# The last mixture of experts: scattered copies of token rows, or token numbers and gathers

## The reference

```python
NUM_EXPERTS, TOP_K, N_GROUPS, N_LIMITED_GROUPS = 32, 6, 4, 2
scores = jax.nn.sigmoid(x @ gate_w)                       # 2048 x 32
# the best 2 of 4 groups of 8 experts, then the best 6 experts in them
_, selected_experts = jax.lax.top_k(masked_scores, K)
weights = take_along_axis(original_scores, selected_experts)
weights = weights / weights.sum(-1)
xs = x_exp[argsort(selected_experts.ravel())]             # 12288 (token, choice) pairs, by expert
g = ragged_dot(xs, w_gate, group_sizes)                   # 256 -> 176
u = ragged_dot(xs, w_up, group_sizes)                     # 256 -> 176
d = ragged_dot(silu(g) * u, w_down, group_sizes)          # 176 -> 256
out = d[unsort_idx].reshape(T, K, H)
expert_out = sum(out * weights[..., None], axis=1)
shared = (silu(x @ sw_gate) * (x @ sw_up)) @ sw_down      # a dense expert, 352 wide, for all tokens
return expert_out + shared
```

## Time and profile before

| what | value |
|---|---|
| median of 3 runs | 3175.97 us (3175.49 to 3180.71) |
| the profiled execution's own time | 3173.69 us |
| its span, from first to last instruction | 3171.7 us |
| mean granted PE clock | 0.891 of full speed |
| busy: PE, DVE, ACT, POOL | 83%, 61%, 49%, 28% of the span |
| last feed-forward: first load issued | 2609.97 us |
| slots ready, first scatter of the dispatch | 2648.88 us |
| last scatter of the dispatch issued | 2769.39 us |
| first transpose of the tile loop | 2820.16 us |
| last addition of products issued | 3143.08 us |
| last DVE addition to x begins, takes | 3159.12 us, 4.43 us |

### The profile page before, as it was taken

The page is one execution under the profiler, slowest core; times in us unless marked ns, Lnnn a source line. Parts: engine busy times, 40 slices in busy tenths (PEclk is TensorE's granted clock), DMA queues, the critical chain, the costliest instruction groups (busy, mean ns, idle before and its releaser), DMA issues. The chain is left out here.

```text
span 3171.7 us, 64439 instructions
## 1 busy us (share of the span) xinstructions
PE 2641.8 (83%) x19747; PEld 2209.5 (70%) x19747; DVE 1937.4 (61%) x5951; ACT 1549.9 (49%) x4650; POOL 901.1 (28%) x800
## 2 busy tenths in 40 slices
PE   6885984899976599999948599999999984279995
PEld 5663553666654499999936499999999982157774
DVE  5666324787762688788843577777777773035553
ACT  6874222899971455555543344444444442013331
POOL 2111784111101322222244201001010114726664
PEclk9995755999986699999979799999999997589998
DMA  6003555900010111010024333332333326446776
GB/s 185 2 14 125 89 93 147 313 2 2 2 42 0 60 41 51 28 57 34 21 111 137 130 105 101 100 104 81 104 101 100 89 67 271 148 113 121 123 125 141
DMA packets 188015, 291.72 MB, mean 92 GB/s; under 512 B 29921, under 2 KB 158105, under 8 KB 183937
## 3 DMA queue, kind: packets, MB, share of 16 engines
q1 hardware_dynamic: 148800, 226.07, 22.2%
q0 software_dynamic: 38976, 62.68, 10.2%
HBM read 110.55 MB, written 94.22 MB: 65 GB/s over the span
## 5 line engine op out<-in xcount | busy, mean ns | idle before, releaser
L584 PE MATMUL bank<-norm_t_high,w 128*128 128x256 f32 (+1 forms) x2176 | 446.8, 287 | 8.3 <-DVE w L766 8.3
L732 ACT ACTIVATE probs<-bank,neg_max 128x256 f32<-128x256 f32 (+1 forms) x512 | 224.9, 444 | 394.0 <-DVE inv L841 385.9
L584 PEld LDWEIGHTS bank<-norm_t_high,w 128*128 128x128 f32 x2176 | 363.2, 194 | 8.9 <-issue 8.9
L1150 ACT ACTIVATE probs<-neg_scores,bound 128x256 f32<-128x256 f32 (+1 forms) x768 | 366.9, 486 | 3.3 <-DVE bound L1221 2.9
L584 PE MATMUL bank<-norm_t_low,w 128*128 128x256 f32 (+1 forms) x1088 | 310.0, 285 | 0.0
L1221 DVE CUSTOM_DVE_ANT_0 neg_scores<-bank,table 128x256 f32<-128x256 f32 (+1 forms) x768 | 261.7, 397 | 63.3 <-PE bank L1062 63.3
L870 POOL TENSOR_TENSOR summed<-turned 128x512 f32<-128x512 f32 x64 | 82.6, 1291 | 710.0 <-DVE turned L792 710.0
L2197 POOL DMA_INDIRECT sums<-shared,norm_t x127 | 198.2, 1560 | 176.1 <-ACT shared L2017 79.7
L642 PE MATMUL bank<-k,q 128*128 128x256 f32 (+1 forms) x1536 | 244.6, 295 | 0.0
L847 DVE SCALAR_TENSOR_TENSOR x_sb<-bank,inv,x_sb 128x256 f32 (+1 forms) x512 | 224.3, 480 | 24.3 <-DVE inv L841 14.1
L740 ACT ACTIVATE probs_t<-bank 128x384 fp32r<-128x384 f32 (+1 forms) x256 | 139.7, 546 | 201.1 <-PE bank L652 200.6
(11 more groups left out here) (394 smaller groups left out, 6012.3 us busy)
## 6 DMA issues: line engine op xcount, KB each, us to landing
z<-norm_t_high SPq DMA_DIRECT2D x96, 256.0 KB, 2.5
z<-norm_t_low SPq DMA_DIRECT2D x96, 256.0 KB, 2.5
rows<-blank SPq DMA_DIRECT2D x1, 21336.0 KB, 65.0
norm_t<-rows SPq DMA_DIRECT2D x127, 168.0 KB
q_turned<-halves SPq DMA_DIRECT2D x256, 64.0 KB
k_turned<-halves SPq DMA_DIRECT2D x256, 64.0 KB
staged<-in_attention SPq DMA_DIRECT2D x12, 1280.0 KB, 6.6
weights<-in_experts SPq DMA_DIRECT2D x1, 13376.0 KB
```

The source lines that it names most:

```text
L584: ins = nc.tensor.matmul(out, stationary(a), moving(c), start=(kt == 0 and m == 0), stop=(kt == n - 1 and m == 2))
L732: ins = nc.scalar.activation(probs[j % 2][:, t, 0:width], s_bank[j % 2][:, score_columns(causal, t)], ACT.Exp, bias=neg_max[j % 2][:, t:t ...
L1150: ins = nc.scalar.activation(probs[q % 2][g][:, t, 0:width], neg_scores[g][:, t, 0:width], ACT.Exp, bias=bound[q % 2][:, g, t:t + 1], scal ...
```

## The change

The last feed-forward gets a stage of its own, `gathered_stage`, in which no token row is copied to its places. The normalised rows, with slot numbers and gates (again 336 floats), are stored once, in token order, by one DMA of SP. One-hot rows are multiplied on PE, as in layer 0, over 127 tiles, and give for each slot the token (`gather_ids`) and the row of the result (`row_ids`, which is choice x 2048 + token; slots without a token get a spare row). Because the row needs the choice too, there are four numbers per tile and not three, and POOL computes the fourth. The shared expert is split: two `shared_up` steps lie before the routing's products on PE, five more and two `shared_down` steps lie between the 16 token tiles of the one-hot products, and five and two come behind. In the loop POOL gathers each tile's rows (six to seven tiles ahead, 8 buffers) and writes products without addition to seven regions of 2048 rows (six choices and a spare one). At the end six results are loaded and added, not two. Fewer expert weights come early (15 of 32 experts, not 22), as the routing's tables are larger; PE waits for the rest only at tile 15. The blank tables of layer 3 are no longer written. The diff, cut:

```diff
-    narrow_attention_stage(core, narrow[1], ..., blanks=scratch[3])
+    narrow_attention_stage(core, narrow[1], ...)
-              3: SparseExperts(32, 6, 176, True, ACT.Silu, "limited", 127, 352, 2, 5)}
+              3: SparseExperts(32, 6, 176, True, ACT.Silu, "limited", 127, 352, True, 12)}
-        sparse_feed_forward(3)
+        gathered_feed_forward(3)
+
+def gathered_stage(core, cfg, router_in, weights_in, shared_in, tables_in, scratch):
+    RING, OUT_RING, AHEAD, MATCHES = 8, 8, 6, 3
+    NUMBERS = 4
+    UP_BESIDE, DOWN_BESIDE = {0: 2, 2: 3, 7: 4, 9: 5, 11: 6}, {4: 0, 13: 1}
+    ACTIVATED_BESIDE, GATED_BESIDE, ADDED_BESIDE = {3: 2, 5: 3, 9: 4, 12: 5, 14: 6}, {4: 2, 6: 3, 10: 4, 13: 5, 15: 6}, {8: 0}
+    def last_steps(up, down):
+        for work, at in ((up, 7), (up, 8), (up, 9), (down, 2), (up, 10), (up, 11), (down, 3)):
+            work(at)
...
+            def _(sp):
+                sp.wait_ge(rows_ready, 1)
+                sp.wait_ge(row_normed, TILES)
+                sp.dma_start(scratch.rows.rearrange("(p t) r -> p t r", p=P), rows).then_inc(table_stored, 16)
+                sp.wait_ge(table_stored, 16)
+                sp.dma_start(weights[:, rows_at:E * W], weights_in[:, rows_at:E * W]).then_inc(weights_loaded, 16)
+                sp.wait_ge(ids_ready, 1)
+                sp.wait_ge(s_y_done, 2 * CHUNKS)
+                sp.dma_start(weights[:, early_weights:rows_at], weights_in[:, early_weights:rows_at]).then_inc(weights_loaded, 16)
+                sp.wait_ge(y_done, NT)
+                for e in range(NT - OUT_RING, NT):
+                    sp.wait_ge(sent_back[e % OUT_RING], landed(e))
+                for k in range(TOP):
+                    sp.dma_start(results[k], ...).then_inc(results_loaded[k], 16)
...
+                # PE
+                for t in range(TILES):
+                    pe.wait_ge(placed, t + 1)
+                    pe.wait_ge(numbered, t + 1)
+                    pe.wait_ge(ordered, t + 1)
+                    for k in range(TOP):
+                        ins = nc.tensor.matmul(ids_bank, of_place[t % MATCHES][:, k, :], of_tile[t % MATCHES][:, :, k, :], ...)
+                    ins.then_inc(sorted_in, 1)
+                    if t in UP_BESIDE:
+                        shared_up(UP_BESIDE[t])
+                    if t in DOWN_BESIDE:
+                        shared_down(DOWN_BESIDE[t])
+                last_steps(shared_up, shared_down)
...
+                # ACT
+                    act.wait_ge(matched, t + 1)
+                    nc.scalar.activation(of_tile[t % MATCHES][:, 0, :, :], of_tile[t % MATCHES][:, 2, :, :], ACT.Copy, scale=columns[:, 0:1])
+                    nc.scalar.activation(of_tile[t % MATCHES][:, 1, :, :], of_tile[t % MATCHES][:, 2, :, :], ACT.Copy, scale=float(t))
...
+                # DVE
+                    need(dve, sorted_in, t - MATCHES + 1)
+                    nc.vector.scalar_tensor_tensor(of_tile[t % MATCHES][:, 2, :, :], ..., ALU.add, ALU.is_equal).then_inc(matched, 1)
+                    nc.vector.tensor_tensor(of_place[t % MATCHES], ..., ALU.is_equal).then_inc(placed, 1)
...
+                # POOL
+                for t in range(TILES):
+                    pool.wait_ge(matched, t + 1)
+                    nc.gpsimd.tensor_tensor(of_tile[t % MATCHES][:, 3, :, :], of_tile[t % MATCHES][:, 2, :, :], order_bf.to_broadcast([P, TOP, NT]), ALU.mult)
+                pool.wait_ge(table_stored, 16)
+                pool.wait_ge(ids_ready, 1)
+                for n in range(NT + AHEAD):
+                    if n < NT:
+                        if n < RING:
+                            pool.wait_ge(s_up_done, SB * (n // KT + 1))
+                        need(pool, product_ready, n - RING + 1)
+                        nc.gpsimd.indirect_dma_start(tile_rows[n % RING], None, scratch.rows, bass.IndirectOffsetOnAxis(gather_ids[:, n:n + 1], 0))
+                    e = n - AHEAD
+                    if e >= 0:
+                        pool.wait_ge(product_ready, e + 1)
+                        nc.gpsimd.indirect_dma_start(scratch.results, bass.IndirectOffsetOnAxis(row_ids[:, e:e + 1], 0), product[e % OUT_RING], None)
```

More of the change, by code:

```diff
@@ L1646, with __init__ @@
 class SparseExperts:
-    def __init__(self, experts, top, hidden, gated, act, router, tiles, shared, sums, crowded):
+    def __init__(self, experts, top, hidden, gated, act, router, tiles, shared, gathers, crowded):
         self.E, self.top, self.H, self.gated, self.act = experts, top, hidden, gated, act
-        self.router, self.tiles, self.shared, self.sums, self.crowded = router, tiles, shared, sums, crowded
+        self.router, self.tiles, self.shared, self.crowded = router, tiles, shared, crowded
+        self.gathers = gathers
         self.width = self.part_width(hidden)
[L1657 to L1661, removed]
+        self.used = C + 1 + 2 * experts if gathers else C + 2
+        self.row = -(-self.used // 16) * 16
+        self.id_at = C
     def part_width(self, hidden):
@@ L1690, in write_blanks @@
         .then_inc(scratch.blank_rows, 16)
[L1691 to L1698, removed]
+    sp.wait_ge(scratch.blank_rows, 16)
+    sp.dma_start(scratch.rows[:, cfg.id_at].rearrange("(i p) -> p i", p=P).bitcast(I32), core.blank_ids[:],
+                 allow_slow_non_contiguous=True).then_inc(scratch.blank, 16)
 class Arena:
@@ L1725, in sparse_stage @@
     nc, x, bank, E, H, TOP = core.nc, core.x, core.bank, cfg.E, cfg.H, cfg.top
-    NT, ROW, W, SUMS, COPIES = cfg.tiles, cfg.row, cfg.width, cfg.sums, cfg.copies
+    NT, ROW, W, COPIES = cfg.tiles, cfg.row, cfg.width, cfg.top
     MOST = TILES
@@ L1743, in sparse_stage @@
     s_gate_bank, s_up_bank = bank[2:4], bank[4:6]
-    sends = [(t, k) for k in range(TOP) for t in range(TILES)] if COPIES > 1 else [(t, k) for t in range(TILES) for k in range(TOP)]
+    sends = [(t, k) for k in range(TOP) for t in range(TILES)]
     PART = len(sends) // PORTIONS
@@ L1807, in sparse_stage @@
             group_chosen = early.take(P, [TILES, GROUPS_OF])
[L1808 to L1811, removed]
+        slots, gates, own = (early.take(P, [TILES, E]) for _ in range(3))
         shared_room = Arena(weights, early_weights) if cfg.crowded else Arena(early.tensor, 0)
@@ L2181, in _ @@
+                for k in range(TOP):
+                    dve.wait_ge(results_loaded[k], 16)
+                    need(dve, result_added, k)
+                    nc.vector.tensor_tensor(x[:], x[:], results[k], ALU.add).then_inc(result_added, 1)
             @block.gpsimd
             def _(pool):
[L2183 to L2191 removed]
@@ L2192, in _ @@
-                for e in range(NT):
-                    pool.wait_ge(product_ready, e + 1)
-                    if SUMS:
-                        need(pool, added[e % LANES], landed(e) - 16)
-                    ids = tile_rows[e % RING][:, ID_AT:ID_AT + 1].bitcast(I32)
-                    nc.gpsimd.indirect_dma_start(scratch.results[e % len(scratch.results)], bass.IndirectOffsetOnAxis(ids, 0), product[e % OUT_RING], None,
-                                                 compute_op=ALU.add if SUMS else ALU.bypass).then_inc(added[e % LANES], 16)
+                pool.wait_ge(order_ready, 1)
```

501 lines of the change are left out of this document (432 added, 69 removed).

## The result

| | before | after |
|---|---|---|
| median of 4 runs each, one chip (us) | 3176.3 | 3206.6 (3197.4 to 3211.5) |
| ratio | | 1.0091, 95% interval 1.0074 to 1.0109 |
| span of the profiled run | 3171.7 | 3206.7 |
| first transpose of the loop | 2820.2 | 2754.1 |
| first transpose to last write issued | 322.9 | 405.3 |

The forecast was 3119. The three stretches are, after against before, -66.1, +82.4 and +18.8 us, together 35.1; forecast were -81.4, +4.8 (+5.4 by this measure) and +20.1. So the loop went wrong, and the front a little.

What follows compares the result with a forecast made beforehand. PE bounds the tile loop at 2.490 us a tile, POOL's 96 scatters and a stall precede it. Front -81.4, loop +4.8, end +20.1 give -56.5: 3173.7 to 3117.2, as median 3119 us; 8 in 10 from 3096 to 3152.

Steps and rivals of the forecast that it cites:

- The pair takes 2.52 to 2.58 ... 4.8 us more: Tile loop: POOL's gather plus write, taken as 2.58 us a tile, barely becomes the bound; 4.8 us more.
- gather 7: Tile loop: starts 10.5 us after the first transpose; gather 126 follows 119 pairs later at +317.5.
- the late weights: Tile loop: last 7.83 MB land at 2769, tile 15 wants them at 2777; cover of 8 us.
- rival 4: Loop: the 22 us stalls come back with POOL issuing without pause; 3180 to 3250 us, chance 0.05.
- The front: Dispatch and shared expert before the loop: scatters and stall go, first transpose from 2820.2 to 2738.8; 81.4 us less.
- The 16 token tiles with the ids: Front: one-hot products from the first match, nine tiles at POOL's pace; 60 us, bounds 48 and 95.
- the six small steps: Front: DVE turns numbers into integers in six small steps, 1.5 us.
- rival 2: Front, slow sorting: DVE and POOL take turns, or PE runs at 1.2 GHz; 3134 us, chance 0.18.
- PE's rest of the shared expert: Front, before the loop: PE goes on at once with five up and two down steps, 28.5 us.
- The first match: Front: after slots are ready at 2647.96, small DVE steps put it at 2650.3.
- The end: After the last write: six results loaded instead of two sums, 20.1 us more, bounds 17 and 25.
- The sign: Whole kernel: faster 0.86, slower 0.10, within 0.2% of before 0.04.

Runs made afterwards that it cites:

- e6: Kernel after with 6.6 of the last 7.83 MB of weights loaded once the ids are ready: 3106.5 us, 0.9983 of before; later 1.0046 on another chip.
- c2: Kernel after, unchanged, run again beside the kernel before on one other chip: 3122.9 us, ratio to before 1.0026.
- c1: Kernel before, unchanged, profiled again on one other chip: 3115.7 us, where the median for before was 3116.1.
- e4: Kernel after with POOL's indirect writes going to consecutive rows, output not the reference's: 3117.9 us, 1.0019 of before.
- e1: Kernel after with products written by SP's queue to consecutive rows, output not the reference's: 3108.6 us, 0.9977 of before.
- fourth and sixth sets: Follow-up comparisons, one chip each: rows or products moved from POOL to SP (before took 3169.6 us); bfloat16 products or 64-row writes (before 3173.5).
- g2: e6 with products written by SP to consecutive rows, POOL only gathering, output not the reference's: 3112.6 us, 0.9828 of before.
- g3: e6 with consecutive rows loaded by SP, POOL only writing, output not the reference's: 3118.8 us, 0.9848 of before.

## Why the prediction was wrong, step by step

**The step that failed is the loop's** ("The pair takes 2.52 to 2.58 ... 4.8 us more"). From the first transpose to the last write issued I had 328.3 us; the trace has 405.3. By the quiet chips' traces this splits into three:
- The pair itself: e6 has 328.2 us. A pair takes 2.57 us in it, as the durations from the earlier trace rows and the gap from the earlier trace rows said. That the sum is right to 0.1 us is partly luck: gather 7 starts at +9.2 and not +10.5, the 119 pairs take 0.8 less, and from the last gather to the last write it takes 12.8 and not 10.8.
- 12.5 us for rows that land late (c2 340.7 against e6 328.2). I had asked whether the late weights themselves come in time for tile 15, and they did; I had not asked what else lands beside them. The gathers for tiles 7 and on are issued in just those 23 us and take up to 14.4 us to land instead of 3.0. PE's one wait for a row is 9.2 of the 12.5 us in c2. That is what one transfer costs another.
- 64.6 us of standing (405.3 against 340.7), which appears only on some chips. That is rival 4, to which I gave 0.05 and 3180 to 3250; it came at 3207. Rival 4 had read the earlier trace rows as belonging to POOL's issue without pause, and I then let layer 0 speak against it. But layer 0's writes add, with 1.59 us each, and the better witness was in the same trace: layer 2's loop, with plain writes every 1.6 us (47 in 74.9 us). It stands too, if less. Its stretch in the kernel before on the first chip, and in c1:

```profile
1700.00:1720.00 20.00, 18.51 (x109) 13.89 (x108) 8.34 (x25) 8.47 (x24) 11.88 (x13) 1.00 0.52 167
```
```profile
1700.00:1720.00 20.00, 19.29 (x119) 14.92 (x118) 9.37 (x27) 9.83 (x27) 12.53 (x14) 1.00 0.57 177
```

The 109 of PE's instructions in 20 us, where a quiet chip has 119, stood in the trace that I had. Layer 2's dispatch is plainer still: between 1640 and 1660 PE is busy for 10.80 us in it, and for 18.19 in c1. I did not look, because layer 2 was not changed.

**The front: -81.4 forecast, -66.1 measured.** 5.4 us were lost ahead of it: the first step on the expert counts comes at 2650.8 instead of 2645.4, and on the quiet chip in both kernels at 2630.7. The 16 token tiles with the ids took 65.6 us instead of 60 (of the 5.6, 1.5 are the six small steps that the prediction priced and left out of its sum; for the rest rival 2's mechanism is at work, at a third of its price or less), and PE's rest of the shared expert 33.3 instead of 28.5, of which 3.4 is a wait behind DVE, which makes the ids first. The first match was 0.6 sooner than forecast. That the stall goes was right. But it was never the kernel's own. It made up 43.7 us of what the front gained; where it isn't, the same change is worth 27.9 us, and POOL's 96 scatters are the bound that is left.

**The end: +20.1 forecast, +18.8 measured.** Six results come 4.9 us apart, as the step said.

**The sign** was right on no chip: +30 us where both kernels stand, +7 (0.26%) where neither does. Over half of the 81 us that the forecast rests on is the removal of a stall whose cause I had written down as unknown; the sum prices its return at nothing, and the chances at 0.05.

## What to carry to other kernels

A stall with an unknown releaser that goes with a rhythm of one engine must be priced twice: as removed where the rhythm goes, and as brought back where the change makes the same rhythm elsewhere. Look for it in parts of the trace that the change doesn't touch. Ask for every large transfer which small ones are in flight beside it, and not only when it lands itself. And run both kernels beside every experiment: without the kernel before at 3114 us, e4 and e1 would have been read as cures. A stage that no kernel changes, as layer 2 here, tells in every trace which kind of chip it is from.

## What the runs showed of the hardware

- Where POOL issues indirect DMAs that don't add every 1.3 to 1.6 us, PE's, ACT's and DVE's waits end late on some chips (in three of the seven comparisons: the first and those of the fourth and sixth sets) and not on others. With whole writes it cost 60 to 65 us in this loop, 43.7 in the dispatch before, and 12 to 19 in layer 2. At one in 2.5 us there is none (g2, g3), and none in layer 0's loop, where every second one adds. Halving rows or bytes of one of the two does not take it away.
- On those chips the profile also loses records: of the 16 increments of a plain write in the loop, mostly 3 or 4 are in the trace of the kernel after, and 16 for 126 of the 127 writes in c2's and 124 in g3's. Records are lost in layer 0's loop too, where nothing stands, so their loss marks the chip and not the wait.
- Why the chips differ, and what path the news shares with POOL's issue, stays open. Each of the six sets had a chip of its own, so the chip is not told apart from the time of its set. Every time here comes with the span of a recorded execution, so no run shows whether the standing is there without the recording.
- POOL's issue of an indirect write costs 0.99 us for 128 rows of 1024 bytes (0.96 without gathers between them, g3), 0.99 for 128 of 512, 0.91 for 64 of 1024, and 1.59 when it adds.
- A gather that takes 3.0 us to land took up to 14.4 beside a contiguous load of 7.83 MB (in e6 up to 16.3, beside the first part of it).
